# Mamba-2 mixer and ternary MLP on one core: looks at low halves regrouped, and per-head columns turned by two full transpositions

## Time and profile before

| | us |
|---|---|
| median of 3 runs | 778.66 |
| lowest, highest | 771.44, 779.11 |
| the profiled execution, whole | 775.15 |
| its span, first to last instruction | 773.3 |
| its mean granted TensorE clock | 0.989 |

### The profile page before, as it was taken

The page is one execution under the profiler, slowest core; times in us unless marked ns, Lnnn a source line. Parts: engine busy times, 40 slices in busy tenths (PEclk is TensorE's granted clock), DMA queues, the critical chain, the costliest instruction groups (busy, mean ns, idle before and its releaser), DMA issues.

```text
span 773.3 us, 20312 instructions
## 1 busy us (share of the span) xinstructions
PE 738.9 (96%) x8486; PEld 609.9 (79%) x8486; DVE 522.8 (68%) x845; ACT 492.1 (64%) x933; POOL 293.0 (38%) x235
## 2 busy tenths in 40 slices
PE   4977999999999999999999998889999999999998
PEld 4855788888887887887888887678888888888887
DVE  6968976986987897797797697873633532642331
ACT  5989878977978977978879888634312321321330
POOL 2073275366457446627707618540010011001002
PEclk9988999999999999999999999999999999999999
DMA  9823144485475277366385369835113003002002
GB/s 300 233 66 110 30 114 118 86 246 133 83 206 175 80 159 215 87 149 195 76 219 184 83 187 320 232 102 159 42 56 109 0 28 136 0 14 91 5 1 84
DMA packets 42299, 94.97 MB, mean 123 GB/s; under 512 B 9888, under 2 KB 15776, under 8 KB 42016
## 3 DMA queue, kind: packets, MB, share of 16 engines
q1 hardware_dynamic: 42208, 93.67, 42.6%
HBM read 84.73 MB, written 17.57 MB: 132 GB/s over the span
## 4 chain that ended last, share of the span: by engine, by line
PE 52%; DVE 22%; ACT 17%; issue 7%; POOL 2%; DMA 1%; SPq 0%; DVEq 0%; ACTq 0%; POOLq 0%
PE ps_y L1691 10%; PE ps_proj L1678 10%; DVE cx L938 7%; PE ps_out L1678 6%; PE ps_x L1678 6%; ACT ring L717 3%; PE ps_proj L1224 3%; DVE ring L993 3%; PE ps_proj L1225 3%; PE ps_proj L1226 3%; ACT ring L721 2%; PE ps_x L1277 2%; PE ps_y L1300 2%; DVE dt_p L913 2%; POOL ring L532 2%
## 5 line engine op out<-in xcount | busy, mean ns | idle before, releaser
L532 POOL TENSOR_TENSOR ring<-tokd,ring 128x1024 f32<-128x1024 f32 x64 | 122.1, 1923 | 177.6 <-ACT tokd L712 124.4
L1224 PE MATMUL ps_proj<-xn_hi,win_x_hi 128*128 128x256 f32 x352 | 104.9, 298 | 2.6 <-DVE xn_lo L907 1.7
L1225 PE MATMUL ps_proj<-xn_lo,win_x_hi 128*128 128x256 f32 x352 | 100.3, 285 | 0.0
L1226 PE MATMUL ps_proj<-xn_hi,win_x_lo 128*128 128x256 f32 x352 | 99.9, 284 | 0.0
L938 DVE SCALAR_TENSOR_TENSOR cx<-cin,consts,cx 128x256 f32<-128x256 f32 x240 | 96.3, 476 | 0.0
L1547 POOL TENSOR_TENSOR res<-res,hidden 128x512 f32<-128x512 f32 (+1 forms) x16 | 20.1, 1257 | 166.3 <-DVE hidden L1610 165.3
L993 DVE TENSOR_TENSOR ring<-ring,ps_tok 128x1024 f32<-128x1024 f32 x64 | 75.6, 1214 | 7.8 <-ACT ring L721 7.6
L1224 PEld LDWEIGHTS ps_proj<-xn_hi,win_x_hi 128*128 128x128 f32 x352 | 67.8, 193 | 15.8 <-issue 12.4
L717 ACT ACTIVATE ring<-ring 128x1024 f32<-128x1024 f32 x64 | 66.8, 1060 | 15.3 <-POOL ring L532 15.3
L1224 PE MATMUL ps_proj<-xn_hi,win_z_hi 128*128 128x256 f32 x256 | 73.9, 289 | 0.0
L1225 PE MATMUL ps_proj<-xn_lo,win_z_hi 128*128 128x256 f32 x256 | 72.3, 282 | 0.0
(11 more groups left out here) (186 smaller groups left out, 1889.9 us busy)
## 6 DMA issues: line engine op xcount, KB each, us to landing
ring<-cum_dram SPq DMA_DIRECT2D x128, 256.0 KB, 5.2
xin<-x SPq DMA_DIRECT2D x8, 512.0 KB, 3.7
res<-x SPq DMA_DIRECT2D x32, 128.0 KB, 2.8
x_dram<-res SPq DMA_DIRECT2D x32, 128.0 KB, 2.9
res<-x_dram SPq DMA_DIRECT2D x16, 256.0 KB, 2.7
out<-res SPq DMA_DIRECT2D x15, 256.0 KB, 2.1
x_in_sb<-x_dram SPq DMA_DIRECT2D x3, 1024.0 KB, 5.6
gate_w_copy<-gate_w SPq DMA_DIRECT2D x4, 704.0 KB, 6.6
```

The costliest lines, as they stand in the source:

```text
L532: pool.tensor_tensor(ring[:, g, :, :], own, ring[:, g, :, :], ALU.subtract).then_inc(diffed, 1)
L1224: pe.matmul(out, hi[:, k, :], xn_hi[:, k, :], start=(k == 0), stop=False)
L1225: pe.matmul(out, hi[:, k, :], xn_lo[:, k, :], start=False, stop=False)
L1226: made = pe.matmul(out, lo[:, k, :], xn_hi[:, k, :], start=False, stop=(k == KT - 1))
```

## The change

Two things, and what hangs on them.

- `dts` becomes two tiles of 128 rows. In `dt_cum` the upper 64 partitions hold DT and the lower 64 CUM, one partition a head, with step, batch and token along the free axis (256 elements); `run_end` holds RUN and TO_END in the same way. `turn_tokd` becomes two full 128x128 transpositions. `make_dt` takes one instruction for each batch, `make_d` and the scan work on 64x256, `make_run` on 64x256 and four times 64x64, and the stores to DRAM read 64 partitions. `make_d` now writes where the scan runs, so that the wait for `cum_out` stands in front of it; ScalarE's wait for `cum_made` in `evacuate(j, 0)` goes.
- The three looks of a block stand together behind `gate(i, 0)` of the same block, in the order 2, 1, 0. Their loads move on SyncE's queue: `low_buf` and `rows` between the ring loads of g 1 and g 2 of step 1, `xin` between those of g 2 and g 3. SyncE's wait at the start of a block is for the looks of the block before, all of which are then in the middle of that block. `low_row` shares the memory of `low_buf`.

```diff
--- before.py
+++ after.py
@@ -128,7 +128,7 @@
         self.scales = sb(ctx, "scales", [P, 2 * MT])
         self.low_max, self.low_all = sb(ctx, "low_max", [P, LOW_PARTS]), sb(ctx, "low_all", [P, 1])
         self.low_buf = sb(ctx, "low_buf", [P, LOW_WIDTHS[2]])
-        self.low_row, self.low_any = sb(ctx, "low_row", [1, P]), sb(ctx, "low_any", [1, 1])
+        self.low_row, self.low_any = self.low_buf[0:1, 0:P], sb(ctx, "low_any", [1, 1])
         self.stats, self.moments = sb(ctx, "stats2", [P, TT, 6]), sb(ctx, "moments2", [P, TT, 2])
         self.spread, self.rstd = sb(ctx, "spread2", [P, TT]), sb(ctx, "rstd2", [P, TT])
         self.minus_half, self.eps = sb(ctx, "minus_half2", [P, TT]), sb(ctx, "eps2", [P, TT])
@@ -179,10 +179,11 @@
         xin = sb("xin", [P, BATCH, HID])
         xres = hand.res
         dt_v, dt_e, dt_p = sb("dt_v", [P, P]), sb("dt_e", [P, P]), sb("dt_p", [P, P])
-        dts = sb("dts", [P, 4, P])
+        dt_cum, run_end = sb("dt_cum", [P, STEPS, BATCH, Q]), sb("run_end", [P, STEPS, BATCH, Q])
+        UPPER, LOWER = slice(0, HEADS), slice(HEADS, P)
         tok = sb("tok", [P, P])
         tokd = sb("tokd", [P, STEPS, 4, HEADS])
-        whole, step_decay = sb("whole", [P, BATCH * HEADS, STEPS]), sb("step_decay", [P, STEPS])
+        whole, step_decay = sb("whole", [P, BATCH * HEADS, STEPS]), sb("step_decay", [HEADS, BATCH, STEPS])
         consts = sb("consts", [P, C_N])
         neg_a = sb("neg_a", [P, 1])
         stats, moments = sb("stats", [P, BATCH, 6]), sb("moments", [P, BATCH, 2])
@@ -191,7 +192,7 @@
         minus_half, eps = sb("minus_half", [P, BATCH]), sb("eps", [P, BATCH])
         ones = sb("ones", [P, 1])
         causal = sb("causal", [P, Q])
-        chain = sb("chain", [P, P])
+        chain = sb("chain", [P, STEPS * BATCH * Q])
 
         def pb(name, banks=1):
             return ctx.enter_context(nc.psum_tensor(name, [P, 512 * banks], F32))
@@ -332,12 +333,12 @@
             def store_cum(i):
                 sp.wait_ge(cum_made, i + 1)
                 for j in range(STEPS):
-                    sp.dma_start(cum_dram[bass.ds(i, 1), j, :, :].rearrange("a r t -> (a r) t"),
-                                 dts[:, CUM, half(j)]).then_inc(cum_out, 16)
+                    sp.dma_start(cum_dram[i, j, :, :].rearrange("(b h) t -> h b t", b=BATCH),
+                                 dt_cum[LOWER, j, :, :]).then_inc(cum_out, 16)
 
             def store_whole(i):
                 sp.wait_ge(step_decayed, i + 1)
-                sp.dma_start(whole_dram[bass.ds(i, 1), :, :].rearrange("a r j -> r (a j)"), step_decay[:]).then_inc(whole_out, 16)
+                sp.dma_start(whole_dram[i, :, :].rearrange("(b h) j -> h b j", b=BATCH), step_decay[:]).then_inc(whole_out, 16)
 
             def load_whole(i, first):
                 sp.wait_ge(whole_out, 16 * i + 16)
@@ -391,7 +392,7 @@
 
             def load_low_rows(i):
 
-                sp.wait_ge(carry_added, STEPS * i + 1)
+                sp.wait_ge(carry_added, STEPS * i)
                 src, width = hand.low_part(3 * (i - 1) + 1)
                 sp.dma_start(rows[:, 0:width], src).then_inc(hand.low_in_parts[1], 16)
 
@@ -411,7 +412,7 @@
 
             def body(i, first, last):
                 if i - 1 in LOOKED:
-                    sp.wait_ge(hand.low_max_made, 3 * (i - 2) + 1)
+                    sp.wait_ge(hand.low_max_made, 3 * (i - 1))
                     if i + 1 < BLOCKS:
                         load_x(i + 1)
                         keep_weights(2 * (i - 2))
@@ -423,8 +424,15 @@
                 if not (first or last):
                     store_x1(i - 1, 0)
                     load_res(i, 0, first)
-                for g in range(GROUPS):
-                    load_cums(i, 1, g)
+                load_cums(i, 1, 0)
+                load_cums(i, 1, 1)
+                if i in LOOKED:
+                    load_low_buf(i)
+                    load_low_rows(i)
+                load_cums(i, 1, 2)
+                if i in LOOKED:
+                    load_low_xin(i)
+                load_cums(i, 1, 3)
                 if first:
                     load_res(i, 0, first)
                 if last:
@@ -432,12 +440,9 @@
                 if not first:
                     store_x1(i - 1, 1)
                 load_res(i, 1, first)
-                if i in LOOKED:
-                    load_low_xin(i)
-                    load_low_buf(i)
-                    if i >= BLOCKS - 3:
-                        keep_weights(COPIES - (BLOCKS - 1 - i))
-                else:
+                if i >= BLOCKS - 3:
+                    keep_weights(COPIES - (BLOCKS - 1 - i))
+                if i not in LOOKED:
                     load_x(i + 2)
                 store_cum(i + 1)
                 store_whole(i + 1)
@@ -445,8 +450,6 @@
                 for g in range(GROUPS):
                     load_cums(i + 1, 0, g)
                 load_whole(i + 1, False)
-                if i in LOOKED:
-                    load_low_rows(i)
                 if i == BLOCKS - 2:
                     sp.wait_ge(projected, EVENTS * i + EVENTS + 6)
                     sp.wait_ge(hand.weights_kept, 16 * COPIES)
@@ -470,7 +473,7 @@
             load_weights(6)
             load_weights(7)
             sp.wait_ge(hand.low_all_made, 1)
-            sp.dma_start(hand.low_row[:], hand.low_all[:]).then_inc(hand.low_in, 16)
+            sp.dma_start(hand.low_row, hand.low_all[:]).then_inc(hand.low_in, 16)
             sp.dma_start(hand.scales[:], mlp_packed).then_inc(hand.scales_in, 16)
             sp.dma_start(hand.scale_d[:], down_s.to_broadcast([P, HID])).then_inc(hand.scales_in, 16)
             store_x1(BLOCKS - 2, 0)
@@ -647,7 +650,6 @@
                     act.wait_ge(dt_abs, j + 1)
                     act.activation(dt_e[:], dt_e[:], ACT.Exp, scale=-1.0).then_inc(dt_exp, 1)
                     act.wait_ge(dt_exp, j + 1)
-                    act.wait_ge(cum_made, j)
                     act.activation(dt_p[:], dt_e[:], ACT.Copy, scale=log_c[-1]).then_inc(soft_step, 1)
                     return
                 if e == 1:
@@ -667,13 +669,13 @@
 
                 act.wait_ge(cum_made, i + 1)
                 act.wait_ge(whole_out, 16 * i)
-                act.activation(step_decay[:], dts[:, CUM, Q - 1::Q], ACT.Exp).then_inc(step_decayed, 1)
+                act.activation(step_decay[:].rearrange("h b j -> h j b"), dt_cum[LOWER, :, :, Q - 1], ACT.Exp).then_inc(step_decayed, 1)
                 act.wait_ge(tokd_turned, STEPS * i)
-                act.activation(dts[:, RUN, :], dts[:, CUM, :], ACT.Exp).then_inc(run_made, 1)
+                act.activation(run_end[UPPER, :, :, :], dt_cum[LOWER, :, :, :], ACT.Exp).then_inc(run_made, 1)
                 for j in range(STEPS):
-                    at = (j + 1) * Q - 1
-                    made = act.activation(dts[:, TO_END, half(j)], dts[:, CUM, half(j)], ACT.Exp, scale=-1.0,
-                                          bias=dts[:, CUM, at:at + 1])
+                    for b in range(BATCH):
+                        made = act.activation(run_end[LOWER, j, b, :], dt_cum[LOWER, j, b, :], ACT.Exp, scale=-1.0,
+                                              bias=dt_cum[LOWER, j, b, Q - 1:Q])
                 made.then_inc(to_end_made, 1)
 
             def first_taps(j, tiles):
@@ -912,22 +914,30 @@
                 dve.wait_ge(soft_step, LOGN * j + n)
                 dve.scalar_tensor_tensor(dt_p[:], dt_p[:], log_c[LOGN - 1 - n], dt_e[:], ALU.add, ALU.mult).then_inc(soft_step, 1)
 
+            def by_step(t, r):
+
+                return t[r, :].rearrange("p (j t) -> p j t", j=STEPS)
+
             def make_dt(j, opening=False):
                 dve.wait_ge(soft_step, LOGN * (j + 1))
                 if not opening:
                     dve.wait_ge(tokd_turned, STEPS * j)
-                dve.tensor_tensor(dts[:, DT, :], dt_v[:], dt_p[:], ALU.add).then_inc(dt_made, 1)
-
-            def make_d(j):
+                for b in range(BATCH):
+                    r = slice(b * HEADS, (b + 1) * HEADS)
+                    made = dve.tensor_tensor(dt_cum[UPPER, :, b, :], by_step(dt_v, r), by_step(dt_p, r), ALU.add)
+                made.then_inc(dt_made, 1)
+
+            def make_d(j, opening=False):
 
                 dve.wait_ge(dt_made, j + 1)
-                dve.tensor_scalar(dt_p[:], dts[:, DT, :], neg_a[:], LOWEST, ALU.mult, ALU.max).then_inc(d_made, 1)
-
-            def make_cum(j, opening=False):
-                dve.wait_ge(d_made, j + 1)
                 if not opening:
                     dve.wait_ge(cum_out, 32 * j)
-                dve.tensor_tensor_scan(dts[:, CUM, :], chain[:], dt_p[:], 0.0, ALU.mult, ALU.add).then_inc(cum_made, 1)
+                dve.tensor_scalar(dt_cum[LOWER, :, :, :], dt_cum[UPPER, :, :, :], neg_a[UPPER, :], LOWEST, ALU.mult, ALU.max).then_inc(d_made, 1)
+
+            def make_cum(j):
+                dve.wait_ge(d_made, j + 1)
```

(22 more changed lines are left out.)

## The result

| | before | after |
|---|---|---|
| median (6 runs each, same chip) | 775.08 us | 790.52 us |
| lowest, highest | 771.44, 779.11 | 785.60, 800.14 |
| profiled execution, span | 775.15, 773.3 | 789.22, 787.4 |

The ratio is 1.0185, with a 95% interval of 1.0144 to 1.0227. Two of the six runs of the changed kernel (800.14 and 799.35) are slow ones and are left out of the ratio. The forecast of 775.4 us (767 to 784) was wrong: the time lies above its range. On the profiled execution the span grew by 14.1 us; the forecast had it shrink by 3.3.

The account below looks back on a forecast made before the run. No engine alone but one block's loop of waits bounds it. Six blocks gain 3.2 us (361.0 against 364.21), block 7 gives 1.3, opening and block 0 cost 1.2: net -3.3, from 778.66 to 775.4 us, range 767 to 784.

Parts of the forecast that it names:

- What bounds the kernel: Mixer blocks 1 to 6: no engine alone; a loop of waits closes block 3 at 59.92 us, VectorE filled for 25.61.
- DMA order: SyncE's queue: copies leave some 8 us earlier; `xin` lands 5 us after issue; 3 us delay of g 2, g 3 free.
- The rivals: Four outcomes beside the 0.50 forecast: 768.8 us (0.20), 780 (0.14), 787 (0.10) and 792 (0.06).
- The look at xin comes late: Mid-block: landing beyond 7.6 us after issue holds VectorE; at 10 us, 11 in all, 787 us; chance 0.10.
- VectorE and GpSimd: They block each other: earlier `diff` meets the normalisation, 17 us in all, 792; three `soft` possibly 1.9 a block; chance 0.06.
- the normalisation: VectorE, ending at 242.19 in block 3: collision with an earlier `diff` would cost 2.8 us a block, 17 in all.
- turn_tokd: TensorE, twice a block: two transpositions for eight products gain 0.39 us each, 0.39 per block on the loop.
- Longer rows on VectorE: `make_dt`, `make_d` and the scan in VectorE's filled stretch: 0.63 us more per block, again before blocks 0 and 1.
- The last block: Block 7: the look at `low_buf` leaves the chain, 0.9 us, and `turn_tokd` gives 0.39; 1.3 gained.
- the two terms: Block 7's gains: 0.9 us from the look at `low_buf` and 0.39 from `turn_tokd`.
- The opening: Before the blocks: longer VectorE rows and ScalarE's extra activations on the chain, 0.63 + 0.6 = 1.2 us with block 0.
- Nothing for make_run: ScalarE, blocks 1 to 6: about 0.6 us more work, counted as nothing because ScalarE waits for VectorE's taps afterwards.

Follow-up runs that it names:

- looks_light: Changed kernel with the three look loads of a block cut to 16 columns each, read repeatedly so VectorE's instructions keep their size; 773.09 us, 0.9992 of before.
- soft_late: Changed kernel with the three `soft` behind `gate_lo` moved behind the mixes of the step; 786.83 us, 1.0187 of before.
- look_rows_twice: Changed kernel whose third look reads `rows` again instead of `xin`, so it waits for nothing; `xin`'s load stays queued; 784.36 us, 1.0133 of before.
- diff_waits: Changed kernel with 16-column look loads, plus a wait of `diff` of g 2 (odd step) for ScalarE's `g_hi`; 784.94 us, 1.0112 of before.
- tiles_only: Kernel before with only the two 128-row tiles and two transpositions, looks and loads unmoved; 780.38 us, 1.0082 of before.
- looks_only: Kernel before with only the looks, their loads, SyncE's waits and `low_row` as in the change; 788.45 us, 1.0228 of before.
- xin_look_next: Changed kernel with only the look at `xin` put back behind `gate_lo` of the next block; 794.09 us, 1.0273 of before.
- rings_first: Changed kernel with SyncE's four ring loads first and the loads of `low_buf`, `rows` and `xin` behind them; 796.37 us, 1.0262 of before.
- after_res: Changed kernel with `load_res(i, 0)` and the two weight copies moved behind all four ring loads; 789.34 us, 1.0192 of before.

## Why the prediction was wrong, point by point

- **What bounds the kernel: right.** The loop of block 3 and its filled stretch held. With light looks the six blocks come to 361.8 us, and the sum forecast 361.0; four of them are 59.97 to 60.02, where 60.16 was forecast, and two are longer.
- **DMA order: this is the step that failed**, in two sentences of it. "I take 5, the value nearest to a load with only one ring pair ahead of it": it is 9.4 us. From the issue of ring g 0 (243.41) to the use of g 3 (261.52) lie 2048 KB of ring and 1408 KB of looks, 3456 KB in 18.1 us. At that rate the looks alone fill 7.4 us (an estimate from these rows); I had named their bytes and not added them up. "So a delay of 3 us is free there": I asked only who waits for `diff` of g 2 and g 3, not what GpSimd would then be running beside. The delay put `diff` of g 3, with the folding of `sq` behind it, on the three `soft`.
- **The rivals.** Both slower mechanisms happened, together, and I gave them 0.16. *The look at xin comes late* decides from 7.6 us, and 9.4 gave waits of 12.8 us in six blocks; as they partly replaced waits for the ring, the piece grew by 2.4 over before and by 8.4 over light looks. *VectorE and GpSimd* came not by the normalisation, the place that I priced, but by the place named only beside it: three `soft`, 1.9 us a block in that sentence, 11.9 us more in six blocks as measured. Taking one link away gave back 0 to 4 us (soft_late) and 4 to 6 (look_rows_twice), and putting the delay of `diff` alone into a kernel without the bytes cost 12 (diff_waits), by medians, or 9 by the ratios, most of it on the eight `soft`. The two don't add up, since a late look moves what VectorE runs beside `diff`; how the 13.8 us divide between them and the clock (below) stays open.
- **The blocking was in the rows of before.** The prediction says that no row of the kernel before shows the three `soft` waiting for `diff`. But the eight `soft` of the same block take 2.57 us in blocks 1 and 5 and 3.22 in 2, 4 and 6, where `fade_state` on GpSimd reaches into them. Block 2 before, VectorE and GpSimd:

```profile
203.58 3.22 DVE L913 SCALAR_TENSOR_TENSOR dt_p<-dt_p,dt_e 128x128 f32<-128x128 f32 x8
200.57 3.79 POOL L550 TENSOR_TENSOR state<-state,whole 128x2048 f32<-128x2048 f32 x1
```

`fade_state` ends at 204.36; eight `soft` of 2.57 begun then would end at 206.93, and they end at 206.80.

- **TensorE's clock: a term that the prediction does not have.** Behind the waits for `xpad` the granted clock fell in blocks 3 and 4, about 2.5 us of the 13.8 (the estimate above). In blocks 1 to 6 of before, looks_light, soft_late and tiles_only it did not fall between `gate_lo` and the scan; in looks_only, look_rows_twice, xin_look_next, rings_first and after_res it fell in one to five blocks each. So part of what either link costs comes by this way, and part of the spread between blocks is this.
- **turn_tokd: right in size, wrong in effect.** The even gate comes 0.5 us sooner (0.39 forecast). But in the kernel before the ring's landing holds `gate_lo` in five of six blocks, and more than half of the gain ends there (tiles_only).
- **Longer rows on VectorE: a little short.** 0.63 forecast, 0.77 measured.
- **The last block: better than forecast,** 2.6 instead of 1.3; the collision of the earlier trace rows is gone with the shifted `diff`. Why it is shorter by more than the two terms is argued, not tested. **The opening:** 1.8 against 1.2 for opening and block 0 together, but one execution can't confirm that: the first odd gate lies anywhere from 101.85 to 107.67 in the ten kernels here with the two tiles (mean 104.4), and from 102.16 to 102.64 in the four with `dts` (mean 102.5).
- **Nothing for make_run:** right. From the first tap behind the scan to the odd gate block 3 takes 15.38 us before and 15.40 after; that piece grew by the scan alone.

## What to carry to other kernels

A DMA that is moved on a queue moves everything behind it: add the bytes between issue and use for every load that is overtaken, at the rate that the queue shows there, before calling a delay free. When a delay is called free because nobody waits for the delayed instruction, look at the timeline for what it will then run beside; here small VectorE instructions with two SBUF inputs waited for what was left of a GpSimd instruction. When TensorE gets a new idle stretch, read its granted clock behind it: here up to five blocks of a kernel ran on at the lower level for some us. And a shorter step in front of a wait for a landing gives nothing until the landing is moved too.

## What was not expected of the hardware

- One GpSimd instruction holds up VectorE instructions of 0.3 us each until it ends: 0.94 us for three became 1.70, and 2.57 for eight became 4.84 (diff_waits, block 2).
- It goes both ways: in the opening of soft_late `wout_lo` takes 4.70 us for two instead of 1.41, and the two `diff` beside it 4.32 instead of 3.77. The opening of kernels with the same code there differs: the first odd gate is at 101.85 in looks_light and at 107.67 in diff_waits. The three slowed pairs of `wout_lo` in diff_waits (3.04, 3.04 and 3.06 us) against two in looks_light (3.06 and 1.91) make up 2.8 of these 5.8 us at most; 2.2 are there at the first `diff` already, and why is not shown.
- A copy of 704 KB between DRAM tensors that leaves right behind four ring pairs, as in the changed kernel, takes 10.7 us to land (`gate_w`, median of four; 6.6 before), with no change in its size.
- Behind an idle stretch of 3.3 us TensorE's granted clock was 0.53 for 3.63 us, and behind one of 3.06 in the block before it stayed at 1.00.
